# Expert blocks of 512 rows with one weight gather each, and results added into the fused rows in DRAM

## The reference, cut to what matters

```python
h = concatenate([tok_ref(x), txt_ref(x_txt)], axis=1)          # 8 x 561 x 192
h = h + attn_ref(layernorm(h))                                 # "fused" in the kernel
x = layernorm(h).reshape(-1, 192)
probs = softmax(x @ gate_w)                                    # 8 experts
top_w, top_i = top_k(probs, 2)
for each row t, each of its two experts e, with weight w:
    y = gelu(x[t] @ w_up[e] + b_up[e]) @ w_down[e] + b_down[e] # 192 -> 768 -> 192
    h[t] += w * y
```

## Time and profile before

| | |
|---|---|
| Median of 3 runs | 4574.51 us (4572.96 to 4578.35) |
| The profiled execution's own time | 4577.79 us |
| Its span in the trace | 4576.1 us |
| TensorE busy | 3883.6 us (85% of the span) |
| VectorE, ScalarE, GpSimd busy | 2267.1, 2207.2, 1206.0 us |
| Attention begins | 2357.1 us |
| Route, place, blocks, combine begin | 3742.8, 3864.2, 3995.2, 4472.9 us |
| SP issues the load of `p_xn` in place | 3869.7 us |

### The profile page before, as it was taken

One profiled execution on the slowest core, in us unless ns is written; L12 is line 12 of the kernel. 1 busy time (PEld: TensorE's weight loads), 2 busy tenths in 40 slices (PEclk: granted clock), 3 DMA queues, 4 the chain that ended last, 5 costly groups with the idle time before them and its releaser, 6 DMA issues. The chain is left out here.

```text
span 4576.1 us, 66931 instructions
## 1 busy us (share of the span) xinstructions
PE 3883.6 (85%) x22252; PEld 2535.1 (55%) x22252; DVE 2267.1 (50%) x3489; ACT 2207.2 (48%) x3426; POOL 1206.0 (26%) x1170
## 2 busy tenths in 40 slices
PE   1799999999999999999849999999999963099990
PEld 1355555555555555555436767667767743078880
DVE  2566666666656666666435444444444422033332
ACT  0355455455545545545516676576666630044540
POOL 4123223323323322332210000010010010644446
PEclk6799999999999999999969999999999985589995
DMA  6423333333333342333011111111111132355554
GB/s 133 119 74 98 110 96 87 115 87 91 104 101 93 98 115 78 89 114 98 26 39 33 25 29 36 25 30 36 29 27 35 29 105 76 74 153 168 162 147 125
DMA packets 307025, 378.69 MB, mean 83 GB/s; under 512 B 64263, under 2 KB 210119, under 8 KB 306631
## 3 DMA queue, kind: packets, MB, share of 16 engines
q1 hardware_dynamic: 270935, 293.64, 23.2%
q0 software_dynamic: 23872, 73.32, 6.2%
q10 hardware_dynamic: 12048, 9.44, 0.6%
HBM read 245.71 MB, written 101.32 MB: 76 GB/s over the span
## 5 line engine op out<-in xcount | busy, mean ns | idle before, releaser
L691 DVE TENSOR_REDUCE mx<-ring 128x2 f32<-128x1024 f32 x768 | 919.5, 1222 | 482.8 <-PE ring L478 479.6
L605 ACT ACTIVATE probs<-ring 128x1024 f32<-128x1024 f32 x768 | 767.6, 1024 | 411.1 <-PE ring L491 410.2
L1421 DVE TENSOR_REDUCE a_nmx<-a_ring 128x1 f32<-128x561 f32 (+1 forms) x480 | 341.7, 737 | 309.0 <-PE a_ring L1270 159.0
L1319 ACT ACTIVATE a_ring<-a_ring,a_nmx 128x561 f32<-128x561 f32 (+1 forms) x480 | 333.8, 695 | 197.9 <-DVE a_nmx L1421 195.3
L1200 POOL TENSOR_SCALAR_AFFINE_SELECT a_probs<-a_probs 128x256 f32<-128x256 f32 (+1 forms) x240 | 91.9, 383 | 1208.7 <-ACT a_probs L1351 1208.7
L478 PE MATMUL ring<-k_stack,q_stack 48*128 48x512 f32 x1536 | 358.1, 477 | 56.4 <-DVE mx L691 24.2
L491 PE MATMUL ring<-q_stack,k_stack 64*128 64x512 f32 x1536 | 357.3, 482 | 54.5 <-DVE mx L691 39.2
L505 PE MATMUL acc<-probs,vals 128*32 128x512 f32 x3072 | 393.9, 633 | 1.3 <-ACT probs L605 1.3
L1351 ACT ACTIVATE a_probs<-a_ring 128x561 f32<-128x561 f32 (+1 forms) x480 | 287.3, 637 | 169.4 <-PE a_ring L1267 166.5
L1267 PE MATMUL a_ring<-a_k_hh,a_q_hl 128*128 128x256 f32 (+1 forms) x960 | 311.2, 339 | 22.9 <-DVE a_q_hl L1401 11.1
L1267 PE MATMUL a_ring<-a_q_hl,a_k_hh 128*128 128x256 f32 (+1 forms) x960 | 287.4, 324 | 10.4 <-ACT a_ring L1319 7.6
(11 more groups left out here) (219 smaller groups left out, 7167.6 us busy)
## 6 DMA issues: line engine op xcount, KB each, us to landing
q_stack<-qk_scratch SPq DMA_DIRECT2D x576, 64.0 KB, 2.4
k_stack<-qk_scratch SPq DMA_DIRECT2D x576, 64.0 KB, 2.4
qk_scratch<-qk_hi SPq DMA_DIRECT2D x32, 768.0 KB, 3.7
qk_scratch<-qk_lo SPq DMA_DIRECT2D x32, 768.0 KB, 5.2
a_q_hm<-a_q_hl SPq DMA_DIRECT2D x48, 280.5 KB
a_k_hh<-a_k_hh SPq DMA_DIRECT2D x48, 280.5 KB
h_in<-tokens SPq DMA_DIRECT2D x34, 384.0 KB, 4.6
res<-tokens SPq DMA_DIRECT2D x32, 384.0 KB, 3.4
```

Source lines behind the costliest of these rows:

```text
L605: nc.scalar.activation(probs[n % 2][:, pair:pair + 2, x // 2, :], buf[:, :, :], ACT.Exp, scale=DK ** -0.5).then_inc(act, 1)
L691: nc.vector.tensor_reduce(mx[s][:, i, :].rearrange("p (r t) -> p r t", r=2)[:, :, t], buf[:, :, :], AX, ALU.max).then_inc(dve, 1)
L1319: nc.scalar.activation(buf, buf, ACT.Exp, bias=nmx[0:r, i, h:h + 1], accum_out=sums[0:r, i, h:h + 1]).then_inc(act, 1)
L1421: nc.vector.tensor_reduce(nmx[0:r, i, h:h + 1], flat(buf)[0:r, 0:N], AX, ALU.max, negate=True).then_inc(dve, 1)
```

## The change

- `BLOCK` is 512, so that there are 25 blocks instead of 44, none of them in a loop. The order of steps is written for one block (`blocks_steps`); `t` and `down` each come twice a block and handle half of it (`down`: two times 128 rows in one PSUM bank), `hi` twice. There are 8 PSUM buffers instead of 6.
- A table in DRAM, `expert_table`, has 128 rows for each expert, each of 2886 floats (11544 bytes): up weights in both parts as the `hi` and `lo` steps want them, down weights, both biases. Seven transfers from DRAM to DRAM write it (11.8 MB), issued by ACT as its first work in attention. A block's weights are then one gather of 128 rows; four tables are held in SBUF.
- Rows in `slots_in` are 208 floats wide: 192 values, the row's token number, its weight, and padding. So `route` fills 10.65 MB (25 transfers of 512 rows) instead of 8.65 MB, each free row with a token number of its own behind the last row of `fused`, and `fused` is padded by 512 rows. `place` loads the normalised rows twice, into the two tiles of the two choices, and no longer makes `expert_rows`.
- In `blocks`, DVE adds the bias, multiplies by the weight, and GpSimd adds the 4 x 128 result rows straight into `fused` by indirect transfers that add; those of block n wait for those of block n-1. `combine` is gone; at the end SP copies `fused` to the output, DRAM to DRAM (3.45 MB).

```diff
@@ attention_phase, ScalarE
             sc.sem_inc(act, BASE)
+            rows = table[:, :].rearrange("(e p) c -> p e c", p=P)
+            up = dram["wup_rows"].rearrange("(e k) (c f) -> c k e f", e=EXPERTS, c=2)
+            for dst, src in ((rows[0:KC, :, 0:FF], up[0]), (rows[KC:P, :, 0:FF], up[1, 0:P - KC]),
+                             (rows[0:D - P, :, FF:2 * FF], up[1, P - KC:KC]), (rows[D - P:P, :, FF:2 * FF], up[1, P - KC:KC]),
+                             (rows[:, :, WDOWN:BDOWN], dram["wdown_rows"].rearrange("(e p) c -> p e c", p=P)),
+                             (rows[:, :, BDOWN:BUP], dram["bdown"].partition_broadcast(P)),
+                             (rows[:, :, BUP:ROW], dram["bup_rows"].rearrange("(e p) c -> p e c", p=P))):
+                sc.dma_start(dst, src).then_inc(made, 16)
             sc.wait_ge(fixed_in, 96)
@@ constants
-BLOCK = 2 * P
+BLOCK = 4 * P
 NBLOCKS = (2 * B * N + EXPERTS * (BLOCK - 1)) // BLOCK
-PLACES = 4
-NBLOCKS += -NBLOCKS % PLACES
+XW = 208
+TABLES, XS = 4, 2
@@ route_phase
+            sp.dma_start(lane[:, :], dram["lane"]).then_inc(lane_in, 16)
             sp.wait_ge(zeroed, 1)
-            sp.dma_start(fused[B * N:P * T_ALL, :], zeros[0:P - R_LAST, 0, :]).then_inc(padded, 16)
+            sp.dma_start(fused[B * N:B * N + BLOCK, :].rearrange("(p i) d -> p i d", i=4), zeros[:, :, 0:D]).then_inc(padded, 16)
...
-            sc.wait_ge(zeroed, 1)
-            sc.dma_start(slots_in[:, :].rearrange("(p n) d -> p n d", p=P),
-                         zeros[:, :, :].to_broadcast([P, NBLOCKS * BLOCK // P, D])).then_inc(filled, 16)
+            sc.wait_ge(zeroed, 2)
+            for n in range(NBLOCKS):
+                sc.dma_start(slots_in[n * BLOCK:(n + 1) * BLOCK, :].rearrange("(p i) d -> p i d", i=4), zeros[:, :, :]).then_inc(filled, 16)
@@ place_phase
-            sp.dma_start(xn[:, :, :], normed[:, :].rearrange("(t p) d -> p t d", p=P)).then_inc(xn_in, 16)
-            sp.wait_ge(done, progress["rows"])
-            sp.dma_start(expert_rows[:, :].rearrange("(n p) k -> p n k", p=P), rows_i[:, :, :]).then_inc(kept, 16)
-            sp.wait_ge(kept, 16)
+            for k in range(2):
+                sp.dma_start(xn[k][:, :, 0:D], normed[:, :].rearrange("(t p) d -> p t d", p=P)).then_inc(xn_in, 16)
@@ blocks_steps
+    ahead = lambda n: [("hi", n, 0), ("hi", n, 1), ("lo", n, 0), ("lo", n, 1), ("t", n, 0), ("t", n, 1)]
+    out = ahead(0)
+    for n in range(NBLOCKS):
+        turn = [("up", n, 0), ("hi", n + 1, 0), ("up", n, 1), ("down", n - 1, 0), ("t", n + 1, 0), ("up", n, 2), ("hi", n + 1, 1),
+                ("lo", n + 1, 0), ("t", n + 1, 1), ("up", n, 3), ("down", n - 1, 1), ("lo", n + 1, 1), ("up", n, 4), ("up", n, 5)]
+        out += [x for x in turn if 0 <= x[1] < NBLOCKS]
+    return out + [("down", NBLOCKS - 1, 0), ("down", NBLOCKS - 1, 1)]
@@ blocks_phase, SyncE
+            for s in (0, 1):
+                sp.wait_ge(scattered[s], 64 * ((NBLOCKS + 1 - s) // 2))
+            flat = lambda t: t.rearrange("r d -> (r d)").rearrange("(p f) -> p f", p=P)
+            sp.dma_start(flat(out_dram[0:B * N, :]), flat(fused[0:B * N, :])).then_inc(stored, 16)
+            sp.wait_ge(stored, 16)
@@ blocks_phase, GpSimd
+            def gather(n):
+                g.indirect_dma_start(table[n % TABLES][:, :], None, table_dram,
+                                     bass.IndirectOffsetOnAxis(ap=which[:, n:n + 1], axis=0)).then_inc(gathered[n % TABLES], 16)
+            for n in range(TABLES):
+                gather(n)
+            for n in range(NBLOCKS):
+                for j in range(2):
+                    g.wait_ge(dve, reached("dve", ("down", n, j)))
+                    if n and j == 0:
+                        g.wait_ge(scattered[(n - 1) % 2], 64 * ((n + 1) // 2))
+                    for i in (2 * j, 2 * j + 1):
+                        g.indirect_dma_start(fused, bass.IndirectOffsetOnAxis(ap=ids[:, n, i:i + 1], axis=0),
+                                             y[n % 2][:, i, :], None, compute_op=ALU.add).then_inc(scattered[n % 2], 16)
+                if n + TABLES < NBLOCKS:
+                    gather(n + TABLES)
@@ blocks_phase, VectorE, step down
+                    nc.vector.tensor_tensor(out, ring[R.buffer[now]][:, 0:2 * D].rearrange("p (i d) -> p i d", i=2), bias,
+                                            ALU.add).then_inc(dve, 1)
+                    v.wait_ge(dve, reached("dve", step) - 1)
+                    share = part[:, n, 2 * m:2 * m + 2].rearrange("p (i a) -> p i a", a=1).to_broadcast([P, 2, D])
+                    nc.vector.tensor_tensor(out, out, share, ALU.mult).then_inc(dve, 1)
```

More of the change, by code:

```diff
@@ L1544, in _ @@
             nc.vector.memset(zeros[:, :, :], 0.0).then_inc(zeroed, 1)
+            v.wait_ge(zeroed, 1)
+            v.wait_ge(lane_in, 16)
+            for i in range(4):
+                ins = nc.vector.tensor_scalar(zeros[:, i, D:D + 1], lane[:, :], 4.0, float(B * N + i), ALU.mult, ALU.add)
+            ins.then_inc(zeroed, 1)
             for s in (ln, xt_done, lg_done, kept):
@@ L1561, in _, with place_phase @@
                 nc.vector.tensor_copy(logits[:, :, :].rearrange("p i e -> p (i e)"), ps_g[:, 0:GT * EXPERTS]).then_inc(lg_done, 1)
[L1564 removed]
+def place_phase(nc, dram, logits_dram, normed, slots_in, which):
     E, T = EXPERTS, T_ALL
@@ L1808, in blocks_phase @@
-        y = each("y", [P, 2, D])
+        table = each(TABLES, "table", [P, ROW])
+        w_hi = each(2, "wup_hi", [P, 2, FF], F32R)
+        w_lo = each(2, "wup_lo", [P, 2, FF], F32R)
+        x = each(XS, "x", [P, 4, XW])
+        ids = sb("m_ids", [P, NBLOCKS, 4], U32)
+        part = sb("m_part", [P, NBLOCKS, 4])
+        x_hi = each(2, "x_hi", [P, 2, BLOCK], F32R)
+        x_lo = each(2, "x_lo", [P, BLOCK], F32R)
+        hid = each(2, "hid", [P, 6, BLOCK])
+        y = each(2, "y", [P, 4, D])
@@ L1813, in blocks_phase @@
+        gathered, x_in = [sem(f"gathered{b}") for b in range(TABLES)], [sem(f"x_in{b}") for b in range(XS)]
+        sems = {"act": act, "dve": dve}
         block = ctx.enter_context(nc.Block())
-        of_block = lambda t, n: t[:, :].rearrange("(n i p) d -> n p i d", p=P, i=2)[n]
-        def per_turn(R, it, each, more):
-            return it * each + (R.turn0 * each + more)
-        def await_step(engine, R, it, name, step, now):
-            value = R.done(it, name, step, now)
-            if value is not None:
-                engine.wait_ge(sems[name], value)
@@ L1826, in _ @@
         @block.sync
         def _(sp):
-            def load(n, b):
-                sp.dma_start(which[b][:, :], expert_rows[:, :].rearrange("(n p) k -> n p k", p=P)[n]).then_inc(which_in[b], 16)
-                sp.dma_start(x[b][:, :, :], of_block(slots_in, n)).then_inc(x_in[b], 16)
-            def steps(R, it):
-                turn = it + R.turn0
-                for now, step in enumerate(R.steps, 1):
-                    if step[0] != "down" or step[2] != 1:
-                        continue
-                    b = step[1]
-                    done = turn - 1 if b == PLACES - 1 else turn
-                    await_step(sp, R, it, "dve", step, now)
-                    sp.sem_inc(tick, 1)
-                    sp.dma_start(of_block(slots_out, done * PLACES + b), y[b][:, :, :]).then_inc(stored[b], 16)
-                    if not (R is R_CLOSE or R is R_FINAL and b < PLACES - 1):
-                        load((done + 1) * PLACES + b, b)
@@ L1909, in _ @@
[L1909 to L1915 removed]
+                last.then_inc(mm, 1)
         @block.scalar
         def _(sc):
[L1919 to L1933 removed]
@@ L1935, in _ @@
-            sc.sem_inc(act, BASE)
-            for R in (R_AHEAD, R_FIRST, R_SECOND):
-                steps(R, 0)
-            with sc.Fori(0, LOOPS) as it:
-                steps(R_LOOP, it)
-            steps(R_FINAL, 0)
+            for now, step in enumerate(R.steps):
+                kind, n, m = step
+                if kind == "hi":
+                    if m == 0:
+                        sc.wait_ge(gathered[n % TABLES], 16 * (n // TABLES) + 16)
+                    nc.scalar.activation(w_hi[n % 2][:, m, :], table[n % TABLES][:, FF * m:FF * m + FF], ACT.Copy).then_inc(act, 1)
+                elif kind == "up":
+                    sc.wait_ge(mm, reached("mm", step))
+                    nc.scalar.activation(hid[n % 2][:, m, :], ring[R.buffer[now]][:, 0:BLOCK], ACT.Gelu,
+                                         bias=table[n % TABLES][:, BUP + m:BUP + m + 1]).then_inc(act, 1)
```

345 lines of the change are left out of this document (105 added, 240 removed).

## The result

| | before | after |
|---|---|---|
| median of the runs (lowest to highest) | 4576.43 us (4572.96 to 4581.62, 4 runs) | 4505.98 us (4503.65 to 4511.67, 4 runs) |
| profiled execution: time, span | 4577.8, 4576.1 us | 4506.42, 4504.5 us |
| ratio of the times, 95% interval | | 0.9839 (0.9827 to 0.9852) |

What follows compares the result with a forecast made beforehand. TensorE was taken to bound the blocks and GpSimd's gathers the matmul-free ending; +2 (blocks), -79.5 (end), +31.6 (attention), +7.5 (route), +2.5 (place), -2 (block start) gave -37.9, so 4537 us, range 4500 to 4562.

Steps and rivals of the forecast that it cites:

- rival 1: Attention: ACT is not held, its seven transfers are taken at once, attention pays only 3 us; 4508 us, chance 0.20.
- rate R: Table transfers and final output copy: DRAM-to-DRAM speed, taken as 229 GB/s, with 180 to 300 considered.
- the formula's 11.0 + 3.0 MB: Head of attention: ACT waits for 11.0 MB of table beside SP's 3.0 MB; 61 us, costing +31.6 us.
- -114.0 + 17.45 MB / R: Whole kernel: summed change in us, with copy and ACT's wait holding 17.45 MB; zero at 153 GB/s.
- thousand rows: Attention's table issues: a queue takes about this many, then the issuing engine waits until the transfer before has gone in.
- Landing of the last scatters: End of the kernel: time before SP issues the output copy, taken as 5 us, between 1 and 7.5.
- Route: Route stage: longer SP issues and the first row load landing later beside a larger fill; +7.5 us, 0 to +20.
- Place: Place stage: a second load of normalised rows and a few small VectorE operations; +2.5 us, 0 to +4.
- The block's 18.07: Block stage: us per 512-row block, summed from parts plus 0.15; 25 blocks take 451.8 us, +2 us.
- The start of the block stage: Start of blocks: GpSimd no longer waits for indices and issues one larger gather instead of five; -2 us, -4 to 0.
- Rival 2: Table and output copy: DRAM-to-DRAM copies are slow; at 120 GB/s the sum is +31, 4606 us; chance 0.07.
- Rival 3: Block stage: adding scatters set the pace, decisive above 4.2 us each; at 5.0 each 4618 us; chance 0.05.

Runs made afterwards that it cites:

- old ending: Changed kernel with results stored in slot order again and the earlier combine stage at the end: 4592.18 us.
- order reversed: Changed kernel with the same seven table transfers in reverse order, biases first and down weights last: 4501.32 us.
- second traces: Kernels run again unchanged for another trace: the changed kernel 4501.31 us, the kernel before 4578.24 us.
- kernel before with the table: Kernel before plus only the seven table transfers in attention and the wait for them, nothing reading the table: 4596.85 us, ratio 1.0037.
- table in place: Changed kernel with the seven table transfers moved from attention to the place stage, behind ACT's exponential: 4494.11 us.

## Why the prediction was right, and where its sizes were off

**The mechanism held.** The ending with GpSimd's 72 gathers went and nothing took its place (the old ending brings back 86 us); TensorE still sets the pace of the blocks (busy 100 of 100 us); ACT pays for the table at the head of attention, where it is held (the order of the issues alone removes it). The time is inside the range, 31 us below the forecast. That it is inside is partly luck: for the mechanism that came true the prediction gave 4512 to 4562, and 4506 lies below that; the range reached down to 4500 only for the sake of rival 1, which was false.

**The step that failed is the rate R**, in two terms. The prediction had no row of a transfer from DRAM to DRAM, only 229 GB/s for loads and 364 for writes, and took the lower because a copy does both. The table moved at 312 to 339, 327 in the mean of the two windows, and the copy of the output at an estimated 336. At 327 the formula's 11.0 + 3.0 MB take 42.8 us, which is where `a_xT` stands (42.7); the prediction counted from 1.4 us into the stage, but ACT's first issue came at 0.06. Put in the sum, -114.0 + 17.45 MB / R gives -60.6 in place of -37.9. The bytes of the formula were near the truth for this order alone: 13.3 MB had moved when ACT was free, and with the order reversed 5.9 where it has 10.1. The queue also took more than the "thousand rows" of the prediction: 1536 in three issues here, 2048 in two with the order reversed.

The 229 was a poor pick even for loads. In the same trace of the kernel before, the load of `p_xn` into SBUF moved 332 GB/s (columns as the earlier trace rows):

```profile
3876.00:3880.00 4.00, 0.00 (x0) 0.00 (x0) 3.90 (x15) 0.00 (x0) 0.00 (x0) 0.50 1.09 332
```

With it in place of 229, both sides of a copy would have stood at 332 and 364. The figure of the Trainium skill that the prediction set beside it (DMA: Bandwidth & Descriptors, Latency and other measured facts, 214 GB/s, measured there on other shapes) points the wrong way here; the trace has 312 to 339. By that figure ACT's delay works out at 36 us and the sum at 5 more, not at 37 and 6.

**Smaller terms.** Landing of the last scatters, 5 taken and 2.1 measured: -3; their issues, 2.3 taken and 3.4 measured: +1. Route +7.5 taken, +2.6 measured: the load with short rows hardly lost against the fill with long ones (13.0 us against 12.3), so the turns that the Trainium skill describes there (DMA: Bandwidth & Descriptors, Queues, rings and completion order) did not cost the short rows what I took. Place +2.5 taken, +0.9 measured. The block's 18.07 was 17.92, the sum of its parts without the 0.15 added: 4 us over 25. The start of the block stage, to the first `up` group, gained 2.4 against 2 (1.4 in the second traces). Not in the sum at all was the clock: some -6 at the start of the blocks, and the +6.6 ahead of attention that goes with it; both lie within what executions differ by.

**The rivals.** Rival 1 (ACT is not held) had 4508 us, the closest number of all to the 4506 measured, and it is false: ACT was held until 2406.25. By the time alone it would have passed for the cause; it took the row "[63.76 <-issue]" and the reversed order to tell. Its 3 us for contention, the later rows, were 0.9 us in the changed kernel and 2.5 in the kernel before with the table (VectorE's wait for `a_tok`), in both hidden under ACT's hold. Rival 2 (slow copies) would have needed 153 GB/s. Rival 3 (adding scatters set the pace) would have needed 4.2 us each and they take 1.7.

**What was not asked.** The prediction priced the 512 rows at +2 and went on; the same sum would have given 43 blocks of 256 rows, 43 x 10.22 = 439, and 31 of 384, with an `up` group halfway between 0.97 and 1.57, 31 x 14.15 = 439: both some 13 us shorter than 451.8. Likewise the hold: by the prediction's own formula ACT waits for every transfer but the last, and so it had in hand that the largest must go last or elsewhere.

## What to carry to other kernels

An engine that issues several large transfers can stand still in its issues while what it issued before moves, here for 42 us over seven issues; put them on an engine that nobody waits for in that stage (12 us gained here), or try the largest last, and look for "<-issue" behind long DMA issues. Before a rate is put in a sum, look for the fastest stretch of its kind in the trace: 229 and 332 GB/s stood in the same one. A stage without matmuls at the end that gathers results can be replaced by adding scatters hidden under the matmuls, at 1.7 us of GpSimd each and a plain copy behind them (13.4 us here). Before larger blocks are taken, work out rows times time per row for the neighbouring sizes: padding may eat what longer instructions save.

## What the runs showed of the hardware

- A transfer from DRAM to DRAM ran at 312 to 339 GB/s with the DMA engines at 1.02; with the table in place it was 345 at 1.03. Loads into SBUF had 229 at 0.99 and 332 at 1.09 (`p_xn`), fills of DRAM with zeros 364 at 1.08 and 389 at 1.03.
- Two transfers of 1024 rows were taken in 0.7 us each by an empty queue, and the next four took 1.3 to 7.8 us; a 24 KB transfer needed 15.5 to 17.6 us to issue behind 4.7 MB and the bias rows. When the issuing engine was free, 2248 to 2433 of the table's 5232 packets were still to move, be it 1.5 or 8.9 MB.
- An adding indirect scatter of 128 rows took GpSimd 1.69 us, the same without adding 1.25.
- From the start of the first `up` group TensorE's clock stayed at half for 4 to 20 us, and for 9 and 18 us in two traces of one program (the kernel before).
- On one chip the kernel before took 4600 to 4616 us in ten runs, 30 more than elsewhere, while the changed kernel took there (4501, 2 runs) what it takes elsewhere; the one with the old ending ran only there and took 4592, as expected from the other chips' times. No trace of the kernel before exists from that chip; the cause is open. Ratios from it (0.9705, 0.9765 and 0.9962) flatter the changed kernels by 0.7%.
